# The opening of a fused state-space and feed-forward layer, put in another order

## The reference, cut to what matters

```python
xn = layernorm(x)                    # x: [2048, 1024] per core
out = x + ssm(xn) + ffn(xn)

def ssm(x):                          # the sum has the residual xn in it
    z = layernorm(x) * ln_gamma + ln_beta
    dt = exp(log_dt); dA = exp(-exp(log_A) * dt[:, None]); dB = B * dt[:, None]
    # for each of 1024 channels d, with 64 states n, over time t
    h[t] = dA * h[t-1] + dB * z[t, d]
    y[t, d] = sum_n C[d, n] * h[t][n] + D[d] * z[t, d]
    return x + y @ W_out.T + b_out

def ffn(x):                          # ternary(w) = round(w / mean|w|) cut to -1, 0, 1
    return gelu(x @ ternary(W1).T + b1) @ ternary(W2).T + b2     # 1024 -> 4096 -> 1024
```

## Time and profile before

| | us |
|---|---|
| median of 3 runs | 597.4 (597.25 to 598.53) |
| the profiled execution | 596.93 |
| its span, first to last instruction, slowest core | 595.0 (cores 593.6 to 595.0) |
| PE, DVE, ACT busy | 576.2, 268.7, 232.4 |
| first `wout` starts | 42.9 |
| first feed-forward matmul starts | 149.8 |

### The profile page before, as it was taken

The page is one execution under the profiler, slowest core; times in us unless marked ns, Lnnn a source line. Parts: engine busy times, 40 slices in busy tenths (PEclk is TensorE's granted clock), DMA queues, the critical chain, the costliest instruction groups (busy, mean ns, idle before and its releaser), DMA issues.

```text
span 595.0 us, 9011 instructions; the slowest of 8 cores (593.6 to 595.0 us)
## 1 busy us (share of the span) xinstructions
PE 576.2 (97%) x3450; PEld 294.5 (49%) x3450; DVE 268.7 (45%) x437; ACT 232.4 (39%) x301; POOL 19.2 (3%) x34
## 2 busy tenths in 40 slices
...
DMA packets 21769, 104.02 MB, mean 175 GB/s; under 512 B 2998, under 2 KB 3382, under 8 KB 14816
## 3 DMA queue, kind: packets, MB, share of 16 engines
...
q10 hardware_dynamic: 300, 0.09, 0.1%
...
## 4 chain that ended last, share of the span: by engine, by line
PE 93%; DVE 2%; issue 2%; ACT 1%; DMA 1%; DVEq 1%; SPq 0%; ACTq 0%
PE pQ L1012 10%; PE pQ L993 9%; PE pY L1012 9%; PE pY L993 9%; PE pW L1012 9%; PE pX L993 9%; PE pW L993 9%; PE pX L1012 9%; PE pW L908 8%; PE pY L884 6%; PE pQ L926 1%; PE pY L891 1%; DMA lBC_s<-abc 1%; PE pX L853 1%; PE pQ L872 1%
## 5 line engine op out<-in xcount | busy, mean ns | idle before, releaser
L1012 PE MATMUL pQ<-w2q,h 128*128 128x512 fp8e4 (+1 forms) x288 | 59.6, 367 | 0.0
L993 PE MATMUL pQ<-xT,w1q 128*128 128x512 bf16 x256 | 57.9, 379 | 0.6 <-DVE w1q L783 0.6
L993 PE MATMUL pY<-xT,w1q 128*128 128x512 bf16 x256 | 57.9, 379 | 0.0
L993 PE MATMUL pW<-xT,w1q 128*128 128x512 bf16 x256 | 57.9, 379 | 0.0
L993 PE MATMUL pX<-xT,w1q 128*128 128x512 bf16 x256 | 57.9, 379 | 0.0
L1012 PE MATMUL pY<-w2q,h 128*128 128x512 fp8e4 x256 | 55.9, 379 | 0.0
L1012 PE MATMUL pW<-w2q,h 128*128 128x512 fp8e4 x256 | 55.9, 379 | 0.0
L908 PE MATMUL pW<-woT,yT 128*128 128x512 bf16 x240 | 54.2, 379 | 0.3 <-ACT yws L548 0.3
L1012 PE MATMUL pX<-w2q,h 128*128 128x512 fp8e4 (+1 forms) x256 | 52.5, 366 | 0.0
L708 DVE TENSOR_TENSOR u<-xn,gm 128x1024 bf16<-128x1024 bf16 x80 | 49.5, 683 | 0.2 <-ACT xn L499 0.2
L1012 PEld LDWEIGHTS pQ<-w2q,h 128*128 128x128 bf16 x288 | 28.1, 97 | 30.7
...
## 6 DMA issues: line engine op xcount, KB each, us to landing
...
```

The lines of the kernel that those rows point to most:

```text
L993: inst = te.matmul(pA[n % 8], w1q8[:, f * 1024 + k * 128:f * 1024 + (k + 1) * 128], x3[:, k, :, :], start=(k == 0), stop=(k == 7))
L1012: inst = te.matmul(out_psum(e, n, cs), h[b][:, f * BT + tk * 128:f * BT + (tk + 1) * 128], w2q8[:, f * 1024 + cs.start:f * 1024 + cs.stop] ...
```

## The change

The work of the opening is the same but for 28 extra matmuls of 128 columns on zeros (`keep_clock`), and its order is another on every engine up to chunk 5; from there the loop is the old one.

- The moment rows come in two groups: `moment(0..3)` first, into `pQ[:, 512:]`, and `mrg` waits for these alone; `moment(4)` and `moment(5)` go to `pQ[0:64, 0:512]` later, with matrices 64 columns wide. `mrow` is copied out in two parts.
- `lBC` is loaded ahead of `lA`, `dte` is made first and `wk[0]` ahead of the exponential of A. The x loads wait for `lBC`. Constants are loaded by SP and ACT in their final form; the 0/1 matrices are written by DVE.
- Chunks 0 to 3 have statistics, roots and finishes of their own (`GROUPS`); from chunk 4 on it is pairs as before. `xn[0]` is made by DVE. For chunks 1 to 3 ACT scales `PP` (`scale_PP`).
- The D product and the tables of a chunk come first, then the other four products, each with its own signal, and `ssm_local` follows product by product. It uses `pW` for chunk 0.
- `ssm_local(0)` runs ahead of the first transpose; `wout(0)` and `wout(1)` run ahead of `ssm_local(2)`; `wout(3)` comes behind `transpose_V(5)`; `xT`, `abs1`, roots and `yW_evict` are laid out by hand up to chunk 5.

The diff, its indent shortened:

```diff
-K_ORDER = [0, 1, NU] + list(range(2, NU))
...
+K_ORDER = [NU] + list(range(NU))
...
+NK = NU + 1
+GROUPS = [[c] for c in range(4)] + [[c, c + 1] for c in range(4, M, 2)]
+GROUP_OF = {c: g for g, cs in enumerate(GROUPS) for c in cs}
...
 def _(sy):
     sy.dma_start(rows[0:2, :], rows_in.ap()).then_inc(d_rows, 16)
+    sy.dma_start(lBC[:, :], abc_in.ap()[:, 512:1536]).then_inc(d_abc, 16)
     sy.dma_start(lA[:, :], abc_in.ap()[:, 0:512]).then_inc(d_lA, 16)
-    sy.dma_start(lBC[:, :], abc_in.ap()[:, 512:1536]).then_inc(d_abc, 16)
-    sy.wait_ge(d_lA, 16)
+    sy.wait_ge(d_abc, 16)
     for c in range(4):
         sy.dma_start(gx[c][:, :],
                      x_in.ap()[c * 128:(c + 1) * 128, :]).then_inc(d_x[c], 16)
+        if c == 0:
+            sy.dma_start(PF[:, :], cP_in.ap()).then_inc(d_PF, 16)
+            sy.dma_start(cQ[:, :], cQ_in.ap()).then_inc(d_tab, 16)
...
+    gp.memset(wv[0][:, :], 0.0)
+    gp.memset(wv[1][:, :], 0.0).then_inc(s_zero, 1)
+    gp.wait_ge(s_zero, 2)
...
-    ac.dma_start(gh[0:2 * NU, :], bass.AP(rows_in, 512, [[0, NU], [RWID, 2], [1, 512]])
-                 ).then_inc(d_gh, 16)
-    ac.dma_start(cC[:, :], cC_in.ap()).then_inc(d_cC, 16)
-    ac.dma_start(par[:, :], par_in.ap()).then_inc(d_par, 16)
     ac.wait_ge(s_cst, 1)
     ac.activation(dump[:, 0:1], cst[:, 0:1], AF.Exp)
...
+    ac.dma_start(sel8f[0:2 * NU, :], cS_in.ap()).then_inc(d_sel, 16)
+    ac.dma_start(gh[0:2 * NU, :], gh_in.ap()).then_inc(d_gh, 16)
+    ac.dma_start(cIDf[:, :], cID_in.ap()).then_inc(d_cid, 16)
+    ac.dma_start(cE[0:64, :], cE_in.ap()).then_inc(d_cE, 16)
+    ac.dma_start(par[:, :], par_in.ap()).then_inc(d_par, 16)
+    ac.wait_ge(s_row, 1)
+    ac.activation(dte[:, :], pY[:, 0:512], AF.Exp).then_inc(s_exp, 1)
     ac.wait_ge(d_lA, 16)
     ac.activation(lA[:, :], lA[:, :], AF.Exp).then_inc(s_exp, 1)
-    ac.wait_ge(s_row, 1)
-    ac.activation(dte[:, :], pY[:, 0:512], AF.Exp).then_inc(s_exp, 1)
...
             ac.wait_ge(s_Q, c - 3)
+            ac.wait_ge(s_u, NK * (c - 3))
...
+    def scale_PP(c):
+        if c == 1:
+            ac.wait_ge(d_PF, 16)
+        ac.wait_ge(s_rs2, GROUP_OF[c] + 1)
+        if c >= 2:
+            ac.wait_ge(s_ssm, c - 1)
+        ac.activation(PP[c % 2][:, :], PF[:, :], AF.Copy, bias=0.0,
+                      scale=rstd2[:, c:c + 1]).then_inc(s_PP, 1)
...
     gm_evict(0)
-    ac.wait_ge(s_mrg, 1)
-    ac.activation(mrow[0:NMR, :], pQ[0:NMR, 512:1024], AF.Copy, bias=0.0,
-                  scale=1.0).then_inc(s_mev, 1)
+    sqrt1(0)
     gm_evict(1)
-    sqrt1(0)
     gm_evict(2)
-    normalise(0)
+    sqrt2(0)
     gm_evict(3)
     gm_evict(4)
-    sqrt2(0)
+    ac.activation(mrow[0:32, :], pQ[0:32, 512:1024], AF.Copy, bias=0.0,
+                  scale=1.0).then_inc(s_mev, 1)
+    xT_evict(0)
+    sqrt1(1)
+    ac.wait_ge(s_mrow, 2)
+    ac.activation(mrow[32:64, :], pQ[32:64, 0:512], AF.Copy, bias=0.0,
+                  scale=1.0).then_inc(s_mev, 1)
+    sqrt2(1)
     normalise(1)
-    xT_evict(0)
+    scale_PP(1)
     VT_evict(0)
     xT_evict(1)
-    sqrt1(1)
+    yT_evict(0)
+    VT_evict(1)
+    sqrt1(2)
+    yT_evict(1)
+    sqrt2(2)
     normalise(2)
-    sqrt2(1)
-    for c in range(M):
+    scale_PP(2)
+    sqrt1(3)
+    VT_evict(2)
+    yW_evict(0)
+    xT_evict(2)
+    sqrt2(3)
+    normalise(3)
+    scale_PP(3)
+    yW_evict(1)
+    yT_evict(2)
+    xT_evict(3)
+    VT_evict(3)
+    abs1(0)
+    yT_evict(3)
+    sqrt1(4)
+    normalise(4)
+    sqrt2(4)
+    yW_evict(2)
+    xT_evict(4)
+    normalise(5)
+    VT_evict(4)
+    abs1(1)
+    yT_evict(4)
+    xT_evict(5)
+    sqrt1(5)
+    normalise(6)
+    sqrt2(5)
+    VT_evict(5)
+    abs1(2)
+    yW_evict(3)
+    xT_evict(6)
+    normalise(7)
+    abs1(3)
+    sqrt1(6)
+    for c in range(5, M):
         yT_evict(c)
         if c + 2 < M:
             xT_evict(c + 2)
...
             VT_evict(c + 1)
         if c + 3 < M:
             normalise(c + 3)
-        if c % 2 == 1 and c // 2 + 2 < 8:
-            sqrt2(c // 2 + 2)
-        if 1 <= c < M - 1:
+        if c % 2 == 1 and c + 3 < M:
+            sqrt2(GROUP_OF[c + 3])
+        if c < M - 1:
             abs1(c - 1)
         if c >= M - 2:
             abs1(c)
-        if c % 2 == 0 and c // 2 + 2 < 8:
-            sqrt1(c // 2 + 2)
-        if c >= 1:
-            yW_evict(c - 1)
+        if c % 2 == 0 and c + 4 < M:
+            sqrt1(GROUP_OF[c + 4])
+        yW_evict(c - 1)
     yW_evict(M - 1)
...
+    dv.memset(cC[:, :], 0.0)
...
+            inst = dv.memset(cC[64 * hf:64 * hf + 64, o + hf:o + hf + 1], 1.0)
+    inst.then_inc(s_cC, 1)
...
-    dv.wait_ge(s_exp, 2)
-    dv.tensor_tensor(lA[:, :], lA[:, :], dte[:, :], ALU.mult)
+    dv.tensor_tensor(rD[0:2, :], rows[0:2, 512:1024], rows[0:2, 1024:1536],
+                     ALU.mult).then_inc(s_rD, 1)
+    dv.wait_ge(s_exp, 1)
     dv.wait_ge(d_abc, 16)
     dv.tensor_tensor(lB, lB, dte[:, :], ALU.mult)
     dv.drain()
     dv.tensor_tensor(wk[0][:, :], lC, lB, ALU.mult).then_inc(s_w, 1)
+    dv.wait_ge(s_exp, 2)
+    dv.tensor_tensor(lA[:, :], lA[:, :], dte[:, :], ALU.mult)
+    dv.drain()
     dv.tensor_scalar(lG[:, :], lA[:, :], LAM0, -TSn, ALU.subtract, ALU.mult)
...
     stats(0)
-    dv.drain()
-    power(4)
-    stats(1)
-    dv.drain()
-    power(5)
-    aggregate(0)
     dv.wait_ge(s_mrow, 1)
     dv.wait_ge(d_gh, 16)
     dv.tensor_tensor(mrg[0:2 * NU, :], pQ[0:2 * NU, 512:1024], gh[0:2 * NU, :],
                      ALU.mult).then_inc(s_mrg, 1)
-    finish_pair(0)
+    dv.drain()
+    aggregate(0)
+    power(4)
+    finish1(0)
+    dv.drain()
+    dv.tensor_scalar(xn[0][:, :], gx[0][:, :], rstd[:, 0:1], sb[:, 0:1],
+                     ALU.mult, ALU.add).then_inc(s_xn, 1)
+    dv.drain()
...
+    def scale_tables(c):
+        if c == GROUPS[GROUP_OF[c]][0]:
+            finish2(GROUP_OF[c])
+        if c == 0:
+            dv.wait_ge(d_PF, 16)
+            dv.wait_ge(d_tab, 16)
+        if c == 0 or c >= 4:
+            dv.tensor_scalar(PP[c % 2][:, :], PF[:, :], rstd2[:, c:c + 1], None,
+                             ALU.mult)
+        dv.tensor_scalar(cQs[c % 2][:, :], cQ[:, c * NR:(c + 1) * NR],
...
+        scale_tables(c)
         for k in K_ORDER:
...
-                         ALU.mult).then_inc(s_u, 1)
+            product(c, k).then_inc(s_u, 1)
...
+    dv.wait_ge(s_gm, 1)
+    product(0, NU)
+    scale_tables(0)
+    dv.drain().then_inc(s_u, 1)
+    for k in range(NU):
+        dv.wait_ge(s_gm, BC_ORDER.index(k) + 1)
+        product(0, k).then_inc(s_u, 1)
+    power(5)
+    stats_group(1)
+    finish1(1)
+    state_factors()
     make_u(1)
-    stats(2)
-    stats(3)
-    dv.drain()
-    aggregate(1)
-    finish_pair(1)
-    finish_pair2(1)
-    for c in range(M):
-        if c % 2 == 1 and c // 2 + 2 < 8:
-            finish_pair(c // 2 + 2)
+    make_V(1)
+    stats_group(2)
+    make_V(2)
+    finish1(2)
+    stats_group(3)
+    make_u(2)
+    finish1(3)
+    make_V(3)
+    make_u(3)
+    stats_group(4)
+    finish1(4)
+    make_V(4)
+    make_u(4)
+    stats_group(5)
+    for c in range(4, M):
+        if c == 4:
+            finish1(5)
+        if c % 2 == 1 and c + 3 < M:
+            finish1(GROUP_OF[c + 3])
         if c + 1 < M:
             make_V(c + 1)
-        if 2 <= c + 1 < M:
             make_u(c + 1)
-        if c % 2 == 0 and c // 2 + 2 < 8:
-            stats_pair(c // 2 + 2)
-        if c % 2 == 1 and c // 2 + 2 < 8:
-            finish_pair2(c // 2 + 2)
+        if c % 2 == 0 and c + 4 < M:
+            stats_group(GROUP_OF[c + 4])
...
     def ssm_local(c):
-        te.wait_ge(s_u, c + 1)
-        if c >= 1:
+        if c == 0:
+            te.wait_ge(s_gm, 3)
+        elif c == 1:
+            te.wait_ge(s_gm, NK)
+        else:
             te.wait_ge(s_yTev, c)
-        for hb in range(2):
-            for k in K_ORDER:
-                for b in range(4 * hb, 4 * hb + 4):
-                    bs = slice(b * 128, (b + 1) * 128)
-                    te.matmul(pY[:, bs], u[c % 2][k][:, bs],
-                              PP[c % 2][:, k * 128:(k + 1) * 128],
-                              start=(k == 0 and b == 4 * hb), stop=False)
+        if 1 <= c < 4:
+            te.wait_ge(s_PP, c)
+        for n, k in enumerate(K_ORDER):
+            te.wait_ge(s_u, NK * c + n + 1)
+            for b in range(8):
+                bs = slice(b * 128, (b + 1) * 128)
+                te.matmul(pS[c][:, bs], u[c % 2][k][:, bs],
+                          PP[c % 2][:, k * 128:(k + 1) * 128],
+                          start=(n == 0 and b % 4 == 0), stop=False)
...
+        if k < NU:
+            inst = te.matmul(pQ[0:32, 512:1024], cC[:, k * 32:(k + 1) * 32],
+                             wk[k][:, :], start=(k == 0), stop=(k == NU - 1))
+        else:
+            o = NU * 32 + (k - NU) * 64
+            inst = te.matmul(pQ[0:64, 0:512], cC[:, o:o + 64], wk[k][:, :],
+                             start=(k == NU), stop=(k == NKX - 1))
+        if k in (NU - 1, NKX - 1):
```

(85 more changed lines are left out.)

154 lines of the change are left out of this document (75 added, 79 removed).

## The result

| | before | after | forecast |
|---|---|---|---|
| median of the runs | 597.95 us (4 runs) | 609.32 us (4 runs) | 603.0, range 596.0 to 607.5 |
| ratio to before, 95% interval | | 1.0183 [1.0148, 1.0218] | |
| profiled execution, and its span | 596.93, 595.0 | 607.92, 605.6 | |

The direction was right, the size was not: 11 us were lost and not 6, and the time lies above the range. One of the four runs of after was disturbed (627 us): it counts in the median and is left out of the ratio, and the other three are 607.9 to 610.5 us.

The account below looks back on a forecast made before the run. PE was taken as the bound, so the opening counts only by shifting the first feed-forward matmul. Queue order 1.6 plus clock 1.1, 2.25 and 1.1 made 6.1 us on 596.93: 603.0 us, range 596.0 to 607.5.

Parts of the forecast that it names:

- The start: Opening up to mrg: lBC first and the clock up by the second moment let mrg start at 12.8, 4.7 us earlier.
- The two waits: PE stands 3.8 us before transpose_V(5) and 3.3 to 3.5 before transpose_V(6); wout(4) starts 1.6 us later than before.
- No later effect: From wout(4) on: both kernels have the same loop, and nothing gives the loss back or adds to it.
- Chunks 0 to 2: From xn[0] to wout(0): ssm_state(0) ends at 30.2, wout(0) starts at 32.6, a lead of 10.3 us.
- The clock: Falls to half rate: 1.1 us for the opening, 2.25 for the first stop, 1.1 for the second.
- the 1.1: Opening, 22.0 to 25.8: PE has only short-column work, half covered by DVE's pace, so 1.1 us for the clock.
- At half clock from chunk 0 on the sum would be 2.7 later: Chunks 0 to 2: alternative in which the array runs at half rate from chunk 0, 2.7 us later.
- taken as nothing: Second half of wout(0): last W_out piece there about 35, asked for at 34.3; up to 1 us, not charged.
- the chunks will be later than this sum by the clock term: At wout(0): reason given for not charging the wait of up to 1 us for W_out.
- The clock at the stops: Before transpose_V(5) and transpose_V(6): the clock falls, 2.25 us at the first, 1.1 at the second.
- C: Opening fails: late lBC +1.2, half-rate moments up to +2.3, half-rate chunk 0 +2.7, W_out +1; 606 to 609, chance 0.14.

Follow-up runs that it names:

- v_first: Changed kernel with make_V(5) ahead of the statistics of chunks 6 and 7 and make_V(6) ahead of finish1(6) in DVE's queue: 602.25 us, 1.0078.
- all3: Changed kernel with the edits of v_first, wo_early and clock_fill together: 601.37 us, ratio 1.0067 to the kernel before.
- b_abc: Kernel before with lBC loaded ahead of lA, dte and wk[0] made first, and x loads waiting for lBC: 602.6 us, 1.0062.
- b_v_abc2: Kernel before with make_V ahead of finish_pair on odd chunks, lBC loaded first, x loads waiting only for the rows: 596.19 us, 0.9975.
- x_early: Changed kernel with x loads waiting for the rows alone, not for lBC: 608.69 us, ratio 1.0188 to the kernel before.
- wo_early: Changed kernel with POOL starting W_out's load when x[0] is there, not x[1]: 606.79 us, ratio 1.0164 to the kernel before.
- clock_fill: Changed kernel with 50 more dummy matmuls in TensorE's waits up to wout(0): 610.65 us, ratio 1.0214 to the kernel before.
- fill_all: Changed kernel with the edits of clock_fill and wo_early, plus 50 dummy matmuls ahead of each of transpose_V(5) and transpose_V(6): 606.35 us, 1.015.

## Why the prediction was right in direction and wrong in size

Right, by its own steps:

- *The start.* `mrg` at 12.4 to 13.0 on six cores (forecast 12.8), and `xn[0]`, 0.81 us long (0.8), done at 15.9 to 16.5 on them (15.9).
- *The two waits.* 3.70 and 3.09 to 3.24 us on cores 2 and 6, for the forecast 3.8 and 3.3 to 3.5; from `ssm_state(4)` to `wout(4)` 16.0 us on core 2 and 16.4 on core 6, for 15.95 (core 6 has rows for 15 of the 16 matmuls of that `wout`, so up to 0.2 of it is a missing row). v_first shows that they are most of the loss. What the step had wrong is whose order it is (above), and that does not change its length.
- *No later effect.* From 150 us on both kernels are dense and equally long.

The step that failed is **"Chunks 0 to 2"** with its term in **"The clock"**, the 1.1. On core 2 everything from `ssm_local(0)` on is late: `ssm_state(0)` 33.99 for 30.2, `wout(0)` 36.86 for 32.6, `ssm_state(4)` 61.88 for 57.3. That is 4.6 us for the 1.1 charged, 4.3 of it there by `wout(0)`. The case "At half clock from chunk 0 on the sum would be 2.7 later" came true on most cores, and chunk 1 fell again. The prediction charged no fall before its stretch of 22.0 to 25.8 and gave no reason for it; the first came at about 17. Core 7 of all3 measured it from the other side. With the clock up to 70 us, `wout(0)` started at 33.40 and `ssm_state(4)` at 58.42, 3.5 us earlier than on core 2 of after both times. So the queue order of the step was right to 0.8 and 1.1 us, and the clock in chunks 0 and 1 cost 3.5 us where 1.1 was charged.

On core 6 the clock cost less in the opening, and W_out, "taken as nothing", took its place. The step had the last piece there at about 35 and asked for at 34.3; it was asked for at 35.6 and there at 38.42. Two things were wrong in it. The 34.3 us of before is the earliest of its eight cores; on the others the last piece landed at 35.5 to 37.4. And the delay of 1.1 us was too small: W_out was issued at 17.25, 5.3 us later than before (POOL's first issue was at 11.90 there). Of that, 0.9 is SP's wait for `lBC`, 0.9 is `PF` and `cQ` between x[0] and x[1], and 3.5 is the longer way from x[1]'s issue to POOL's. b_abc showed the wait for `lBC` on the old kernel, where b_v_abc2 mended it; x_early, which takes it away here, brought the issue only to 15.0 to 16.2. But an issue 6 us earlier moved the landing by 1.2 us on average (wo_early), so the late issue explains only a part of the wait; what sets the landing, no run told apart. The lead that should have been kept ran into it: 2.99 us and then a fall of the clock (0.50 from 40 to 46 us). The sentence "the chunks will be later than this sum by the clock term" holds on the cores where the clock fell. It makes the two losses alternatives, not independent: core 6 of after and core 4 of clock_fill, with the early `wout(0)`, met W_out, and the cores with the late one did not.

The clock at the stops was charged 3.35 us. At the first the clock held on five cores, at the second it fell on all and cost 1.7 on most (5.30 for 3.6 us of `wout(4)`). Core 3, where it fell at both, paid 1.7 and 2.6. The Trainium skill (TensorE: Matmul & The Clock Gate, "HAM oscillation — how this bites in real kernels") has each such stop pay for the way up again; the trace agrees at the stop of 3.09 us, and at the longer one of 3.70 it does not on five of the eight cores. One reading of a row was off too: before, the clock was back at 41.6 and not 41.4, 5.9 us after work resumed; the sum does not use it.

The sum for core 6, from these rows: `wout(4)` starts at 80.55 for 71.67, +8.9, and the first feed-forward matmul at 160.63 for 149.84, +10.8. Against the forecast's 6.1 that is +5.8 in chunks 0 to 3 (`ssm_state(4)` at 64.19 for 57.3, less the 1.1), +0.4 up to `wout(4)`, and 1.45 less for the clock at the stops: 4.7 in all.

Of the rivals, C was the nearest in place and size (chunk 0 at half rate and W_out on top, 606 to 609), and I gave it 0.14. Two of its parts came: the clock in chunk 0, and W_out, priced at 1 us and 2.99 on core 6. The other two did not (`lBC` landed at 5.75 on core 6 and the four moments took 4.1 us there). That its range nearly holds the result is in part luck. I held it too unlikely, since I added its parts as mishaps instead of asking which of them the early start itself brings.

What stays open: why the clock is back by 20 us on two cores and not on the six others with the same program; what made the halt in fill_all; what sets the landing of W_out; and why b_v_abc2 gives nothing for its earlier first loads.
